# Transposing DMAs in place of fp32 TensorE transposes in a recurrent layer with routed experts

## The chip, the core and the metric

The kernel runs on one core of a Trainium2 chip. The metric is the device time of one execution in microseconds (us); lower is better. Engines are named as in the profile: PE is TensorE's matmul stream, PEld its weight loads, DVE is VectorE, ACT ScalarE, POOL GpSimd, SP SyncE. SPq, POOLq and ACTq are the instructions by which these engines issue DMAs.

## What is computed

4096 tokens (8 sequences of 512) of 256 channels are normalised. One branch is a linear recurrence with a gate, the other a mixture of 8 experts with the best two of them per token; the output is the input plus the product of the two.

```python
xn = _layernorm(x, axis=-1)
# recurrent branch, per sequence
q, v = xn @ Wq, xn @ Wv
new = sigmoid(beta) * prev + v_t            # over the 512 steps
y = layernorm(q * states) * ln_g + ln_b
s = (y * silu(xn @ Wg)) @ Wo
# expert branch
logits = xn @ router_weight.T; top 2 of 8, gates = softmax(top_vals)
o_e = (silu(a) * b) @ w_out[e].T            # a, b = split(xn @ w_in[e].T)
g = silu(sum_e gate_e * o_e + bias)
out = x + s * g
```

## The kernel before, in words

Every matmul on data runs in fp16 pairs: a number is split into a high half and a low half (value minus high half), and the helper `three` (L1067) issues high*high, high*low and low*high into the same PSUM bank. A matmul needs its operand with channels on the partitions, so token rows have to be transposed somewhere.

**Routing stage.** SP loads x in 8 groups of 4 tiles of 128 tokens into `xst` (L308), then the first four pieces of the expert weights (`load_w(0)`, L317), then it fills `y_dram` with the bias (L321, L323). Per group, DVE takes statistics (`stats_x`), POOL the reciprocal root (`rstd`), ACT normalises into `rows`, a buffer of 260 fp32 words a token: 256 channels and 4 words of data on the routing (`norm_x`, L566). PE transposes the rows of a group in fp32 by 8 matmuls with the identity into bank A or B (`transpose_x`, L1082), ACT casts the bank to fp16 into `xnT` (`high_xt`, L573), DVE subtracts to get the low half (`low_xt`, L745), and PE computes the logits (`route_x`, L1090). `xnT` is also the operand of the three projections of the recurrence. DVE's program has `choose(0)` (L769 to L782) and the split of the projection weights (L824) between the low halves of groups 4 and 5, and `count(0)` and `place(0)` between those of groups 5 and 6; after group 7 comes `choose(1)`, and then the recurrence.

**Recurrence.** Eight steps, one per sequence. POOL scatters the rows meanwhile to `slots_dram`, a list per expert, one indirect DMA per tile and choice (64 of them, L454): 14 at first, then 8 per step. SP brings the rest of the expert weights, ACT and DVE split them in high and low halves.

**Experts.** 32 blocks of 256 slots of one expert each (pairs), then 7 blocks of 128 (singles). For block b, SP waits until the buffer is free, reads the block's row number from `blk_row`, and loads 260 KB from `slots_dram` into `slot_in` (`load_slots`, L348). PE transposes the block in fp32, 4 matmuls with the identity into bank D (`transpose_slots`, L1195); ACT casts to fp16 (`high_slots`, L659), DVE makes the low half (`low_slots`, L978). PE's order for a pair is in `one_block`: first half of the hidden layer into bank A, the transposes of the next block, second half into bank B, then the output matmuls of the block before into bank C; 24 matmuls each. ACT (L667, L672) and DVE (L984, L988) make the activations between them. DVE multiplies the outputs by the gates (`gate_y`, L1003), POOL adds them to `y_dram` by indirect DMAs (L524), where each block's scatter waits until the one before has landed, since two blocks can hold the same token. POOL reads the routing words of each block in `meta` (L478 to L490).

**End.** When all scatters have landed SP loads `y_dram` (L380), ACT applies silu, DVE multiplies and adds, SP stores.

Of the kernel before, what the change touches and what calls it, by code (L numbers as in the profile page):

```python
# [33 lines left out]
P = 128  # L34
B, S, D = 8, 512, 256
T = B * S
NT = T // P
KD = D // P
TPC = S // P
CH = B  # L40
# [61 lines left out]
def build(nc, x, wq, wv, wg, wo, beta, ln_g, ln_b, router, w_exp, bias, out):  # L102
    ctx = ExitStack()
    with ctx:
# [19 lines left out]
        rows = rows_raw[:, :].rearrange("p (t r) -> p t r", r=ROW)  # L124

# [31 lines left out]
        slot_in = [part(rows_raw, SB * ROW).rearrange("p (s r) -> p s r", r=ROW) for _ in range(2)]  # L157
# [83 lines left out]
        slots_ps = [bankD[:, i, :].rearrange("p (k n) -> p k n", k=KD) for i in range(2)]  # L241
# [6 lines left out]

        first_slots_ps = [bankB[:, i, :].rearrange("p (k n) -> p k n", k=KD) for i in range(2)]

        def slots_ps_of(b, i):
            return first_slots_ps[i] if isinstance(b, int) and b < 2 else slots_ps[i]
# [11 lines left out]
        xt_ps, xt_hi_ready, xt_lo_ready = map(sem, ("xt_ps", "xt_hi_ready", "xt_lo_ready"))  # L264
# [14 lines left out]
        slot_t_ps, slot_hi_ready, slot_lo_ready, h_ps, y_ps, y_sb = map(  # L279
            sem, ("slot_t_ps", "slot_hi_ready", "slot_lo_ready", "h_ps", "y_ps", "y_sb"))  # L280
# [14 lines left out]
        slots_v = slots_dram.rearrange("(n p) r -> p n r", p=P)  # L295
        w_exp_v = w_exp.rearrange("p (n w) -> p n w", w=PIECE)
# [5 lines left out]
        def _(sp):  # L302
# [39 lines left out]
            def load_slots(b, i):  # L342
                if not isinstance(b, int) or b >= 2:
                    sp.wait_ge(slot_t_ps, b - 1)
                if not isinstance(b, int) or 2 <= b < PAIRS + 2:
                    sp.wait_ge(meta_ready, b - 1)
                row = sp.value_load(blk_row[0:1, bass.ds(b, 1)], min_val=0, max_val=E * REGION // P)
                sp.dma_start(slot_in[i][:, 0:units(b), :], slots_v[:, bass.ds(row, units(b)), :])\  # L348
                  .then_inc(slot_loaded[i], 16)

            def two(b):
# [10 lines left out]
                if isinstance(b, int) and b == X_EARLY + 1:  # L362
                    for n in range(SINGLES):
                        row = sp.value_load(blk_row[0:1, PAIRS + n:PAIRS + n + 1], min_val=0,
                                            max_val=E * REGION // P)
                        sp.dma_start(one_in[:, n:n + 1, :], slots_v[:, bass.ds(row, 1), D:ROW])\
# [21 lines left out]
        def _(pool):  # L388
# [83 lines left out]
            def meta(b, i, first):  # L472

                pool.wait_ge(slot_loaded[i], b * 8 + 16 if i == 0 else b * 8 + 8)
# [3 lines left out]
                pool.tensor_tensor(is_first[i][:, :], slot_in[i][:, :, D], e_b, ALU.subtract)\  # L478
# [7 lines left out]
                pool.tensor_tensor(gate_c[i][:, :], slot_in[i][:, :, D + 1], is_first[i][:, :], ALU.mult)\  # L486
                    .then_inc(pool_step, 1)
                pool.wait_ge(pool_step, b * 3 + n_meta + 3)
                pool.tensor_tensor(gate_c[i][:, :], gate_c[i][:, :], slot_in[i][:, :, D + 2], ALU.add)
                pool.tensor_copy(dest_f[i][:, :], slot_in[i][:, :, D + 3]).then_inc(meta_ready, 1)  # L490
# [56 lines left out]
        def _(act):  # L547
# [13 lines left out]
            def norm_x(g):  # L561
# [3 lines left out]
                for j in range(g * TPC, (g + 1) * TPC):  # L565
                    last = act.activation(rows[:, j, 0:D], xst[:, j, :], ACT.Identity,  # L566
# [15 lines left out]
            norm_x(0)  # L582

            act.wait_ge(cols_loaded, 48)
            act.activation(cols[:, 3, :], cols[:, 0, :], ACT.Tanh, scale=0.5).then_inc(lam_th, 1)
            for g in range(1, CH):
                norm_x(g)
                high_xt(g - 1, 1 - g % 2)
# [6 lines left out]
            high_xt(CH - 1, 1)  # L595
# [30 lines left out]
            def recur(c, convert=True, last=False):  # L626
# [10 lines left out]
                if last:  # L637
# [14 lines left out]
            def high_slots(b, i, first):  # L652
# [3 lines left out]
                elif not first:  # L656
                    act.wait_ge(h_ps, b * 2 - 2)
# [676 lines left out]
```

## Time and profile before

| | us |
|---|---|
| three runs | 511.03, 509.99, 511.35 |
| median of the runs | 511.03 |
| profiled execution: span from the first to the last instruction | 509.6 |
| PE busy in the span | 426.3 (84%) |
| POOL busy | 268.0 (53%) |
| DVE busy | 307.9 (60%) |
| ACT busy | 214.4 (42%) |

The profile gives the span of its execution; the time of that execution with what lies around the span is not listed apart, and the runs lie 0.4 to 1.8 us above the span. Rows of the trace are read so: start, duration, engine, line of the code, operation, output<-input, shape, count; in square brackets the idle time of the engine just ahead, and what ended it. For a DMA the row of the issuing engine is the time of the issue; the landing is given apart.

### The profile page before, as it was taken

The page shows a single profiled execution, that of the slowest core. Times are in us where ns is not written, and L with a number is a line of the kernel's source. Part 1 is how long each engine was busy: PE and PEld are TensorE (multiplying, and loading weights), DVE is VectorE, ACT ScalarE, POOL GpSimd, SP SyncE. Part 2 cuts the span into 40 slices and gives each one's busy share as a digit, 9 for nine tenths or more (in the row PEclk, how much of TensorE's full clock was granted, in tenths as well). Part 3 has the DMA queues.
Part 4 walks back from the last instruction along what each step waited for, and adds up shares of the span by engine and source line. Part 5 has one row for each costly group of instructions (what it writes and reads, how often), then busy time and mean ns, then how long its engine had stood idle before and what let it go on. Part 6 is the DMA issues. An engine that isn't in the chain of part 4 may idle for free.

```text
span 509.6 us, 12045 instructions
## 1 busy us (share of the span) xinstructions
PE 426.3 (84%) x3446; PEld 337.1 (66%) x3447; DVE 307.9 (60%) x605; ACT 214.4 (42%) x340; POOL 268.0 (53%) x501
## 2 busy tenths in 40 slices
PE   1757795998898899998999989999999999997000
PEld 1644352665557798887888878888888888664000
DVE  4898999899965545464445444545454545443077
ACT  4873273777756433333324233424342423232060
POOL 4726775788762055555555464646564655633200
PEclk9999997999999999999999999999999999999655
DMA  8892366566923226645434343434343434342498
GB/s 250 297 354 93 90 241 220 175 235 231 327 89 85 84 45 144 144 63 106 60 62 62 62 62 62 57 67 62 62 62 62 62 62 54 68 58 25 75 351 302
DMA packets 52692, 64.70 MB, mean 127 GB/s; under 512 B 5552, under 2 KB 47536, under 8 KB 52656
## 3 DMA queue, kind: packets, MB, share of 16 engines
q1 hardware_dynamic: 37712, 45.55, 29.1%
q0 software_dynamic: 13296, 17.83, 20.9%
q10 hardware_dynamic: 1664, 1.06, 0.7%
q8 instruction: 10, 0.16, 0.1%
q14 instruction: 10, 0.08, 0.0%
HBM read 40.02 MB, written 28.74 MB: 135 GB/s over the span
## 4 chain that ended last, share of the span: by engine, by line
PE 38%; DMA 18%; DVE 16%; issue 14%; POOL 8%; ACT 2%; SPq 2%; DVEq 1%; POOLq 1%; ACTq 0%
PE bankC L1071 14%; PE bankB L1071 12%; DMA y_dram<-rows_raw 11%; PE bankA L1071 8%; POOL slots_dram L454 4%; DMA rows_raw<-slots_dram 4%; PE bankD L1195 2%; DMA w_raw<-x_in 2%; DVE rows_raw L1003 2%; POOL stat L418 1%; DVE w_raw L918 1%; DVE w_raw L1049 1%; DVE work L909 1%; DVE bn L935 1%; DMA w_raw<-y_dram 1%
## 5 line engine op out<-in xcount | busy, mean ns | idle before, releaser
L524 POOL DMA_INDIRECT y_dram<-rows_raw x71 | 113.2, 1595 | 50.1 <-issue 31.1
L1071 PE MATMUL bankC<-w_raw,rows_raw 128*128 x852 | 99.5, 273 | 2.3 <-DVE rows_raw L1041 2.1
L1071 PEld LDWEIGHTS bankC<-w_raw,rows_raw 128*128 128x128 f16 x852 | 81.9, 98 | 14.2 <-issue 3.5
L454 POOL DMA_INDIRECT slots_dram<-rows_raw,pos_i x64 | 74.1, 1158 | 31.1 <-issue 20.2
L1071 PE MATMUL bankA<-rows_raw,w_raw 128*128 128x256 f16 x768 | 89.1, 273 | 1.2 <-DVE rows_raw L978 1.2
L1071 PE MATMUL bankB<-rows_raw,w_raw 128*128 128x256 f16 x768 | 89.1, 273 | 0.0
L1071 PEld LDWEIGHTS bankA<-rows_raw,w_raw 128*128 x768 | 75.1, 98 | 10.1 <-issue 1.4
L1071 PEld LDWEIGHTS bankB<-rows_raw,w_raw 128*128 x768 | 75.2, 98 | 8.3
L988 DVE TENSOR_TENSOR rows_raw<-rows_raw 128x512 f16<-128x512 f32 x64 | 44.3, 693 | 45.6 <-ACT rows_raw L672 45.6
L984 DVE SCALAR_TENSOR_TENSOR rows_raw<-rows_raw,bankA 128x512 f32<-128x512 f32 x32 | 22.0, 688 | 73.6 <-ACT rows_raw L667 73.6
L667 ACT ACTIVATE rows_raw<-bankA 128x512 f32<-128x512 f32 x32 | 19.1, 596 | 101.2 <-PE bankA L1071 101.2
L672 ACT ACTIVATE rows_raw<-rows_raw 128x512 f16<-128x512 f32 x64 | 40.3, 630 | 49.6 <-DVE rows_raw L984 49.6
L518 POOL TENSOR_TENSOR spare<-spare 128x1 f32<-128x1 f32 x32 | 6.2, 192 | 95.6 <-DVE rows_raw L1003 94.6
L1003 DVE TENSOR_SCALAR rows_raw<-bankC,rows_raw 128x256 f32<-128x256 f32 x71 | 31.4, 480 | 11.7 <-DMA y_dram<-rows_raw 9.4
L984 DVE SCALAR_TENSOR_TENSOR rows_raw<-rows_raw,bankB 128x512 f32<-128x512 f32 x32 | 22.0, 688 | 15.6 <-ACT rows_raw L667 15.5
L667 ACT ACTIVATE rows_raw<-bankB 128x512 f32<-128x512 f32 x32 | 19.1, 597 | 22.0 <-PE bankB L1071 22.0
L918 DVE SCALAR_TENSOR_TENSOR w_raw<-work,w_raw 128x1024 f32 (+1 forms) x24 | 27.7, 1214 | 0.0
L978 DVE TENSOR_TENSOR rows_raw<-bankD,rows_raw 128x512 f16<-128x512 f32 (+1 forms) x37 | 23.5, 634 | 2.5 <-ACT rows_raw L659 2.4
L1195 PE MATMUL bankD<-ident,rows_raw 128*128 128x128 f32 x134 | 21.4, 278 | 3.5 <-DMA rows_raw<-slots_dram 2.9
L1071 PE MATMUL bankC<-wat_hi,work 128*128 128x256 f16 x128 | 22.3, 273 | 1.8 <-DVE work L963 1.4
L645 ACT ACTIVATE work<-bankD,stat 128x256 f32<-128x256 f32 x32 | 15.4, 564 | 19.5 <-POOL stat L419 19.5
L478 POOL TENSOR_TENSOR rows_raw<-rows_raw,blk_e 128x2 f32<-128x2 f32 x32 | 23.5, 735 | 0.0
(181 smaller groups left out, 640.6 us busy)
## 6 DMA issues: line engine op xcount, KB each, us to landing
work<-w_exp_in SPq DMA_DIRECT2D x24, 512.0 KB, 5.0
rows_raw<-slots_dram SPq DMA_DIRECT2D x32, 260.0 KB, 2.8
w_raw<-x_in SPq DMA_DIRECT2D x9, 512.0 KB, 4.5
y_dram<-bias_in SPq DMA_DIRECT2D x4, 1024.0 KB, 12.7
w_raw<-y_dram SPq DMA_DIRECT2D x8, 512.0 KB, 7.4
out<-w_raw SPq DMA_DIRECT2D x8, 512.0 KB, 3.8
work<-x_in SPq DMA_DIRECT2D x7, 512.0 KB
slots_dram<-fill SPq DMA_DIRECT2D x9, 260.0 KB, 5.7
```

Of the source, the lines that this page charges most:

```text
L454: pool.indirect_dma_start(out=slots_dram, out_offset=bass.IndirectOffsetOnAxis(slot, 0), in_=row, in_offset=None, bounds_check=SLOTS - 1, ...
L478: pool.tensor_tensor(is_first[i][:, :], slot_in[i][:, :, D], e_b, ALU.subtract)\
L524: pool.indirect_dma_start(out=y_dram, out_offset=bass.IndirectOffsetOnAxis(to, 0), in_=ys[i][:, s, :], in_offset=None, bounds_check=ROWS_O ...
L667: act.activation(sil[j][:, :, 0:n], AB[j][:, :, 0:n], ACT.Silu, scale=1.0 / WSCALE).then_inc(sil_ready, 1)
L672: act.activation(g_hi[i][:, 2 * j:2 * j + 2, 0:n], g32[j][:, :, 0:n], ACT.Copy)\
L918: dve.scalar_tensor_tensor(w_lo[:, piece], wst[:, i % STAGES, :], WSCALE, w_hi[:, piece], ALU.mult, ALU.subtract).then_inc(w_lo_ready, 1)
L978: dve.tensor_tensor(xT[i][:, KD:2 * KD, 0:n], slots_ps_of(b, i)[:, :, 0:n], xT[i][:, 0:KD, 0:n], ALU.subtract).then_inc(slot_lo_ready, 1)
L984: dve.scalar_tensor_tensor(g32[j][:, :, 0:n], sil[j][:, :, 0:n], 1.0 / WSCALE, AB[j][:, :, BLOCK:BLOCK + n], ALU.mult, ALU.mult).then_inc( ...
L988: dve.tensor_tensor(g_lo[i][:, 2 * j:2 * j + 2, 0:n], g32[j][:, :, 0:n], g_hi[i][:, 2 * j:2 * j + 2, 0:n], ALU.subtract).then_inc(g_split, 1)
L1003: last = dve.tensor_scalar(ys[i][:, s, :], bankC[:, i, s * D:s * D + D], gates[:, s:s + 1], None, ALU.mult)
L1071: last = pe.matmul(out_ap, lhsT, rhs, start=(n == 0), stop=(n == len(todo) - 1))
L1195: last = pe.transpose(slots_ps_of(b, i)[:, k, s * P:s * P + P], slot_in[i][:, s, k * P:k * P + P], ident32[:, :])
```

## The change

Three edits that go together.

1. **Rows hold fp16 halves.** `norm_x` normalises `xst` in place. ACT (`high_x`) casts a group to fp16 into the first 256 halfwords of its rows, DVE (`low_x`) writes the low half into the next 256. A row keeps its 260 words, so the scatters move the same bytes.
2. **The projections' operand.** For each of the 8 groups SP waits for `low_x` and issues four transposing DMAs from the rows into `xnT`, 128 rows of 512 halfwords each (32 DMAs). PE's fp32 transposes and the casts out of PSUM are gone. The DMAs stand on SP between `load_w(0)` and the fills of `y_dram`.
3. **The expert blocks.** `load_slots` waits until the hidden layer of the block two before is done, and issues one transposing DMA from `slots_dram` straight into the operand `xT`, both halves; a second small DMA brings the 4 routing words (`meta_in`), for which SP waits for `meta` of the block two before. `transpose_slots`, `high_slots` and `low_slots` are gone.

```diff
+        rows16 = rows_raw[:, :].bitcast(F16).rearrange("p (t r) -> p t r", r=2 * ROW)
...
-        slot_in = [part(rows_raw, SB * ROW).rearrange("p (s r) -> p s r", r=ROW) for _ in range(2)]
+        meta_in = [part(rows_raw, SB * META).rearrange("p (s r) -> p s r", r=META) for _ in range(2)]
...
@@ sync
             load_w(0)
+
+            for g in range(CH):
+                sp.wait_ge(x_lo_ready, g + 1)
+                for j in range(TPC):
+                    sp.dma_start_transpose(xnT[:, g, :, j * P:j * P + P], rows16[:, g * TPC + j, 0:2 * D])\
+                      .then_inc(xt_loaded[g], 16)
+
             for t in range(0, NT, 2 * TPC):
...
             def load_slots(b, i):
-                if not isinstance(b, int) or b >= 2:
-                    sp.wait_ge(slot_t_ps, b - 1)
-                if not isinstance(b, int) or 2 <= b < PAIRS + 2:
-                    sp.wait_ge(meta_ready, b - 1)
-                row = sp.value_load(blk_row[0:1, bass.ds(b, 1)], min_val=0, max_val=E * REGION // P)
-                sp.dma_start(slot_in[i][:, 0:units(b), :], slots_v[:, bass.ds(row, units(b)), :])\
+                if isinstance(b, int) and b >= PAIRS + 2:
+                    sp.wait_ge(one_h_ps, b - PAIRS - 1)
+                elif not isinstance(b, int) or b >= 2:
+                    sp.wait_ge(h_ps, b * 2 - 2)
+                n = units(b) * P
+                row = sp.value_load(blk_row[0:1, bass.ds(b, 1)], min_val=0, max_val=E * REGION)
+                sp.dma_start_transpose(xT[i][:, :, 0:n], slots16[bass.ds(row, n), 0:2 * D])\
                   .then_inc(slot_loaded[i], 16)
+                if not isinstance(b, int) or b < PAIRS:
+                    if not isinstance(b, int) or b >= 2:
+                        sp.wait_ge(meta_ready, b - 1)
+                    sp.dma_start(meta_in[i], slots_dram[bass.ds(row, BLOCK), D:ROW]
+                                 .rearrange("(s p) r -> p s r", p=P)).then_inc(meta_loaded[i], 16)
...
@@ scalar
-                    last = act.activation(rows[:, j, 0:D], xst[:, j, :], ACT.Identity,
+                    last = act.activation(xst[:, j, :], xst[:, j, :], ACT.Identity,
...
-            def high_xt(g, i):
-                act.wait_ge(xt_ps, g + 1)
-                act.activation(xnT[:, g, 0:KD, :], AB[i][:, :, :], ACT.Copy).then_inc(xt_hi_ready, 1)
+            def high_x(g):
+                act.wait_ge(x_norm, g + 1)
+                tiles = slice(g * TPC, (g + 1) * TPC)
+                act.activation(rows16[:, tiles, 0:D], xst[:, tiles, :], ACT.Copy).then_inc(x_hi_ready, 1)
...
@@ vector
-            def low_xt(g, i):
-                dve.wait_ge(xt_hi_ready, g + 1)
-                dve.tensor_tensor(xnT[:, g, KD:2 * KD, :], AB[i][:, :, :], xnT[:, g, 0:KD, :],
-                                  ALU.subtract).then_inc(xt_lo_ready, 1)
+            def low_x(g):
+                dve.wait_ge(x_hi_ready, g + 1)
+                tiles = slice(g * TPC, (g + 1) * TPC)
+                dve.tensor_tensor(rows16[:, tiles, D:2 * D], xst[:, tiles, :], rows16[:, tiles, 0:D],
+                                  ALU.subtract).then_inc(x_lo_ready, 1)
...
@@ tensor
             def route_x(g):
-                pe.wait_ge(xt_lo_ready, g + 1)
+                pe.wait_ge(xt_loaded[g], 16 * TPC)
...
             def one_block(b, i, last=False):
                 off = weights_at(b)
-                pe.wait_ge(slot_lo_ready, b + 1)
+                slots_here(b, i)
                 hidden(b, i, 0, off, False)
-                if not last:
-                    transpose_slots(b + 1, 1 - i, False)
                 hidden(b, i, 1, off, False)
                 outputs(b - 1, 1 - i, weights_at(b - 1), False)
```

SP's queue at the start of the program, before (the loads of x stand ahead of these rows):

```order
L317 DMA work<-w_exp_in 128x1024 x4
L321 DMA y_dram<-bias_in 128x8x256 x4
L323 DMA y_dram<-bias_in 16x2048
L317 DMA work<-w_exp_in 128x1024 [waits w_lo_ready] x8
```

and now (the pair of rows L321 stands eight times, once per group):

```order
L314 DMA work<-w_exp_in 128x1024 x4
L321 DMA_TRANSPOSE xs_raw<-rows_raw 128x4x128 [waits x_lo_ready]
L321 DMA_TRANSPOSE xs_raw<-rows_raw 128x4x128 x3
L321 DMA_TRANSPOSE xs_raw<-rows_raw 128x4x128 [waits x_lo_ready]
L321 DMA_TRANSPOSE xs_raw<-rows_raw 128x4x128 x3
```

Thirty-two DMAs with eight waits on DVE stand now ahead of the fills of `y_dram` and of all later loads.

PE's loop over the pairs, at the end of the first half of the hidden layer (bank A) and the start of the second (bank B), before:

```order
L1071 MATMUL bankA<-rows_raw,w_raw 128x256
L1190 ISA
L1195 MATMUL bankD<-ident,rows_raw 128x128 [waits slot_lo_ready,slot_loaded1]
L1195 MATMUL bankD<-ident,rows_raw 128x128 x3
L1071 ISA [waits g_ready]
L1071 MATMUL bankB<-rows_raw,w_raw 128x256 x2
```

and now:

```order
L1053 ISA
L1053 MATMUL bankA<-rows_raw,w_raw 128x256
L1053 ISA [waits g_ready]
L1053 MATMUL bankB<-rows_raw,w_raw 128x256 x2
L1053 ISA
```

The four transposes and their wait for a load are gone from the middle of the block; PE waits for `slot_loaded` once, ahead of the first half.

SP's loop over the pairs, one block, before:

```order
L347 ISA [waits meta_ready,slot_t_ps]
L347 TENSOR_LOAD blk_row
L347 ISA x2
L348 ISA
L348 DMA rows_raw<-slots_dram 128x2x260
```

and now:

```order
L352 ISA [waits h_ps]
L352 TENSOR_LOAD blk_row
L352 ISA x2
L353 ISA
L353 DMA_TRANSPOSE rows_raw<-slots_dram 128x4x256
L357 REGISTER_ALU
L358 ISA [waits meta_ready]
L358 DMA rows_raw<-slots_dram 128x2x4
```

The load no longer waits for POOL, but for PE's second half of the hidden layer two blocks before; the wait for POOL stands behind it, ahead of the small load.

## Rows read from the trace of the kernel before

**Rows 1.** The page: the span.
```profile
span 509.6 us, 12045 instructions
```
**Rows 2.** Windows: stretch; length, busy us (instructions) of PE, PEld, DVE, ACT, POOL; clock; DMA.
```profile
10.60:42.90 32.30, 22.90 (x207) 17.69 (x208) 28.84 (x86) 23.59 (x38) 14.07 (x40) 1.00 0.84 278
42.90:57.90 15.00, 11.05 (x49) 4.84 (x48) 13.93 (x50) 4.91 (x6) 11.34 (x13) 0.89 0.28 100
181.10:428.20 247.10, 243.44 (x2205) 214.87 (x2203) 122.95 (x203) 85.20 (x146) 139.43 (x320) 1.00 0.43 72
470.90:509.60 38.70, 0.00 (x0) 0.00 (x0) 18.83 (x17) 8.46 (x8) 3.11 (x2) 0.56 0.80 241
```
**Rows 3.** Timeline of PE, one pair in the middle of the experts.
```profile
343.45 0.60 PE L1195 MATMUL bankD<-ident,rows_raw 128*128 128x128 f32 x4
343.89 2.78 PE L1071 MATMUL bankB<-rows_raw,w_raw 128*128 128x256 f16 x24
346.51 2.78 PE L1071 MATMUL bankC<-w_raw,rows_raw 128*128 x24
349.13 2.78 PE L1071 MATMUL bankA<-rows_raw,w_raw 128*128 128x256 f16 x24
351.87 0.66 PE L1195 MATMUL bankD<-ident,rows_raw 128*128 128x128 f32 x4
```
**Rows 4.** Chain that ended last (start, us, what): bank B of blocks 2 and 31.
```profile
181.12 2.62 PE bankB L1071 x24
...
428.21 2.62 PE bankB L1071 x24
```
**Rows 5.** Timeline of POOL, the scatter of one pair, then that of block 30.
```profile
350.39 0.19 POOL L518 TENSOR_TENSOR spare<-spare 128x1 f32<-128x1 f32 x1 [2.11 <-DVE rows_raw L1003]
...
353.40 1.58 POOL L524 DMA_INDIRECT y_dram<-rows_raw  x1 [0.31 <-issue]
...
434.45 0.19 POOL L518 TENSOR_TENSOR spare<-spare 128x1 f32<-128x1 f32 x1 [1.91 <-DVE rows_raw L1003]
```
**Rows 6.** Instructions by tile y_dram: time from issue to landing of its DMAs.
```profile
DMA to landing us min/median/max: 3.6/3.9/14.1
```
**Rows 7.** Timeline of SP: the first load behind the last scatter of the experts.
```profile
482.17 7.12 SPq L380 DMA_DIRECT2D w_raw<-y_dram  x8
```
**Rows 8.** Timeline of PE at the first blocks: transposes of blocks 0 and 1, first hidden matmuls.
```profile
157.08 1.04 PE L1195 MATMUL bankB<-ident,rows_raw 128*128 128x128 f32 x8
...
159.31 2.79 PE L1071 MATMUL bankA<-rows_raw,w_raw 128*128 128x256 f16 x24 [1.19 <-DVE rows_raw L978]
```
**Rows 9.** Instructions of L348 (duration ns min/median/max): SP's block loads, 260 or 130 KB.
```profile
L348 SPq DMA_DIRECT2D rows_raw<-slots_dram x39: 337/381/400, 152.6 to 452.2; - x39
...
DMA to landing us min/median/max: 2.1/2.8/3.1
```
**Rows 10.** Waits of SP's queue: engine, line, waited for: us, times, longest.
```profile
SPq L346 <- POOL rows_raw L490: 213.7, 30, 11.7
```
**Rows 11.** Timeline of SP at the start.
```profile
17.99 2.52 SPq L317 DMA_DIRECT2D work<-w_exp_in  x4
20.55 12.09 SPq L321 DMA_DIRECT2D y_dram<-bias_in  x4
```
**Rows 12.** Timeline of the routing stage: choose(0), low halves of groups 5 to 7, last logits.
```profile
28.81 0.41 DVE L769 TENSOR_REDUCE w_raw<-bankD 128x128 f32<-128x256 f32 x1
35.57 1.21 DVE L745 TENSOR_TENSOR xs_raw<-bankB,xs_raw 128x1024 f16<-128x1024 f32 x1
39.93 1.22 DVE L745 TENSOR_TENSOR xs_raw<-bankA,xs_raw 128x1024 f16<-128x1024 f32 x1
41.07 1.21 DVE L745 TENSOR_TENSOR xs_raw<-bankB,xs_raw 128x1024 f16<-128x1024 f32 x1
42.34 0.56 PE L1090 MATMUL bankD<-rt,xs_raw 128*128 128x16 f16 x16 [0.57 <-DVE xs_raw L745]
```
**Rows 13.** Timeline of POOL: one scatter of rows to the slots.
```profile
42.36 0.98 POOL L454 DMA_INDIRECT slots_dram<-rows_raw,pos_i  x1 [0.30 <-issue]
```

More of the change, by code:

```diff
@@ L263, in build @@
         bn_done, x_var, x_rstd, x_norm = map(sem, ("bn_done", "x_var", "x_rstd", "x_norm"))
[L264 removed]
+        x_hi_ready, x_lo_ready = sem("x_hi_ready"), sem("x_lo_ready")
+        xt_loaded = [sem(f"xt_loaded{g}") for g in range(CH)]
         logits_done, route_step, chosen_ready, ranks_done = map(
@@ L650, in recur @@
                     keep_s(c)
-            def high_slots(b, i, first):
-                act.wait_ge(slot_t_ps, b + 1)
-                if isinstance(b, int) and b >= PAIRS + 2:
-                    act.wait_ge(one_h_ps, b - PAIRS - 1)
-                elif not first:
-                    act.wait_ge(h_ps, b * 2 - 2)
-                n = units(b) * P
-                act.activation(xT[i][:, 0:KD, 0:n], slots_ps_of(b, i)[:, :, 0:n], ACT.Copy)\
-                   .then_inc(slot_hi_ready, 1)
             def half(b, i, j, before):
@@ L673, in half, with halves @@
                    .then_inc(g_hi_ready, 1)
-            def halves(b, i, before, last=False):
+            def halves(b, i, before):
                 half(b, i, 0, before)
-                if not last:
-                    high_slots(b + 1, 1 - i, before == 0)
                 half(b, i, 1, before)
@@ L1005, in gate_y, with halves @@
                 last.then_inc(y_sb, 1)
-            def halves(b, i, last=False):
+            def halves(b, i):
                 half(b, i, 0)
-                if not last:
-                    low_slots(b + 1, 1 - i)
                 half(b, i, 1)
-            low_slots(0, 0)
-            low_slots(1, 1)
             half(0, 0, 0)
@@ L1074, in _ @@
             pe.wait_ge(consts, 2)
-            def transpose_x(g, i):
-                pe.wait_ge(x_norm, g + 1)
-                if g >= 2:
-                    pe.wait_ge(xt_lo_ready, g - 1)
-                for j in range(TPC):
-                    for k in range(KD):
-                        last = pe.transpose(AB[i][:, k, j * P:j * P + P],
-                                            rows[:, g * TPC + j, k * P:k * P + P], ident32[:, :])
-                last.then_inc(xt_ps, 1)
             def route_x(g):
-                pe.wait_ge(xt_lo_ready, g + 1)
+                pe.wait_ge(xt_loaded[g], 16 * TPC)
                 for j in range(TPC):
@@ L1187, in weights_at, with slots_here @@
                 return pe.value_load(blk_off[0:1, bass.ds(b, 1)], min_val=0, max_val=(E - 1) * EW)
-            def transpose_slots(b, i, first):
+            def slots_here(b, i):
                 pe.wait_ge(slot_loaded[i], b * 8 + 16 if i == 0 else b * 8 + 8)
-                if not first:
-                    pe.wait_ge(slot_lo_ready, b - 1)
-                for k in range(KD):
-                    for s in range(units(b)):
-                        last = pe.transpose(slots_ps_of(b, i)[:, k, s * P:s * P + P],
-                                            slot_in[i][:, s, k * P:k * P + P], ident32[:, :])
-                last.then_inc(slot_t_ps, 1)
             def hidden(b, i, j, off, first):
```

82 lines of the change are left out of this document (28 added, 54 removed).

## The prediction, made before the changed kernel ran

> **What bounds the kernel now.** I read the windows by stage first. In the routing stage, 10.6 to 42.9 us, DVE is busy 28.8 of 32.3 us and PE 22.9; nothing is full, the stage is a relay through all engines. In the pairs, 181.1 to 428.2 us, PE is busy 243.4 of 247.1 us: half of the span (509.6 us) is PE alone [rows 1, 2]. The timeline of PE shows what it does there: three groups of 24 matmuls that follow each other at 2.62 us (343.89, 346.51, 349.13), then four transposes, then the next group [rows 3]. The chain of waits runs through these groups; between bank B of block 2 and that of block 31 lie 428.21 - 181.12 = 247.1 us, 29 blocks of 8.52 us [rows 4]. Three groups make 7.86 us, so transposes and what they wait for cost 0.66 us a block. Behind the pairs POOL decides: from the moment it takes up the scatter of block 30 (434.45) to the first load of the end (482.17) lie 47.7 us of scatters that wait for each other [rows 5, 7].
>
> **What the change takes away from the experts.** The four transposes of a pair go, with the wait for the load in the middle of the block, and the cast and subtraction behind them on ACT and DVE, which are off the path. If PE then runs group after group, 29 blocks x 0.66 = **19.1 us** go. At the first blocks PE transposes from 157.08 and starts the hidden layer at 159.31 [rows 8]; without the transposes it can start at once, 2.2 us earlier, and the two transposes ahead of bank B of block 2 (0.44 us each in the pitch of rows 3) go too: **3.1 us**. From block 30 on nothing is gained, since the scatters do not change: the 7 transposes of the singles are worth nothing while POOL's chain is the later one.
>
> What must hold for this. (a) The load of a block is now late by two conditions of its own: it starts when the hidden layer of the block two before is done, and must have landed when PE comes to its first half, that is after an output group, two hidden groups and an output group, 4 x 2.62 = 10.5 us. A plain load of these bytes lands 2.8 us after its issue [rows 9]; SP must also read the row number. Slack about 7 us. (b) SP waited 214 us for `meta` in these loads [rows 10]. That wait now stands behind the transposing DMA, and behind it only the small load of routing words and the next block's load are queued. The two DMAs per block cost SP twice 0.38 us instead of once, out of time that it spends waiting. (c) POOL's scatter of a pair begins at 350.39, issues its second DMA at 353.40, which lands 3.9 us later: 6.9 us before the next scatter can begin [rows 5, 6]. That fits under 7.86 us, by 1.0 us.
>
> **What it costs in the routing stage.** The casts and subtractions stay, 1024 elements a partition, now out of SBUF instead of PSUM; a subtraction took 1.21 us [rows 12] and I take the same. The fp32 transposes of PE go, but what stands in their place is on the path: 32 DMAs on one queue. SP is not free for them before 17.99 + 2.52 = 20.5 us [rows 11], where PE could transpose a group as soon as it was normalised. Call T the time by which a transposing DMA of 128 KB holds the queue. No row shows one. From below: SP issues a plain DMA in 0.38 us [rows 9]. From above, the dearest issue of 128 rows in the trace: POOL's indirect DMA, 0.98 + 0.30 = 1.28 us [rows 13]. The nearest by queue and bytes is the first; but a transposition must be cut into many more pieces than a copy of rows, as an indirect DMA is, so I take the middle, **T = 0.8 us**, and keep both ends.
>
> The relay then runs as follows; 2.1 us is the landing of 130 KB [rows 9], 1.7 us of it behind the issue. Low halves of groups 0 to 3 are ready by the time SP reaches them. 16 DMAs end at 20.5 + 16T, with landing and `route_x` (0.56 us [rows 12]) the logits of the first half are there at 22.8 + 16T = 35.6 us. Then DVE's order decides: today `choose(0)` starts at 28.81 and the low halves of groups 5, 6 and 7 end at 36.78, 41.15 and 42.28, that is 7.97, 12.34 and 13.47 us later [rows 12]; now they end at 43.6, 47.9 and 49.1. Group 5's four DMAs take SP from 43.6 to 46.8, group 6's from 47.9 to 51.1, group 7's to 54.3; with 1.7 + 0.6 the last logits are there at 56.6 us instead of 42.90. **+13.7 us**, and the recurrence begins that much later. With T = 0.38 the same sums give 46.6 (+3.7), with T = 1.28 they give 68.9 (+26.0).
>
> Behind SP's waits stand the fills of `y_dram` (12.1 us of issue [rows 11]) and the second piece of the expert weights. The fills are needed at the first scatter of the experts, 100 us later; the weights wait for DVE, which comes later as well. Both at nothing; cover gone, the fills would delay the weights by a few us.
>
> **The clock.** PE has little left to do in the routing stage. Where it idled at the end of the program, the granted clock was 0.56 on average; in 42.9 to 57.9 us, with 11.05 us busy of 15, it was 0.89 [rows 2]. Were that stretch run at the lower level (1.2 GHz, 0.5), PE's 11.05 us would become 11.05 x 0.89 / 0.5 = 19.7, 4.7 more than the stretch. Most of it lies beside `choose(1)` on DVE: I take **+1.5 us**, from 0 to 4.7.
>
> **Sum.** 509.6 - 19.1 - 3.1 + 13.7 + 1.5 = 502.6 us of span. The profiled execution's span lies 1.4 us under the median, so **504.0 us** against 511.03. The change balances a sure gain against an unknown T: it breaks even where the routing stage loses 22.2 - 1.5 = 20.7 us, at T = 1.1 us.
>
> The Trainium skill speaks on both sides. Its page "Advanced Engine Details and Errata", section "X-Bar Transpose (TRN2)", says that transposing DMAs are as fast as ordinary ones; by that T would be that of the plain issue, and the sum 493. Its page "DMA: Bandwidth & Descriptors" gives, in a table of the sequencer's own time, 631 cycles for a transpose out of HBM against 512 for a copy in earlier generations, but for a transpose out of SBUF one push per tile, so that its price grows with the data; it does not say there how large a tile is, so it gives no time here. That second rule speaks against exactly the 32 DMAs out of SBUF, not against the blocks, and no row here shows either.
>
> **The rivals.**
> 1. *SP becomes the bound of the routing stage.* If the queue takes a transpose out of SBUF piece by piece, T is over 1.1 us and all 32 stand in line on the path. It decides from T = 1.1. At T = 1.28: 509.6 - 22.2 + 26.0 + 1.5 + 1.4 = 516; at T = 1.6 (logits at 77.9, +35.0) 525; at 2.0 (89.1, +46) 536. For it: the issue of 128 single rows already costs 1.28 us on POOL. Against: SP's plain issue costs the same 0.38 us for 130 and 260 KB [rows 9]. Chances 0.22 up to 525, 0.08 beyond. The skill's table of the sequencer's time is the rule that would bring this about.
> 2. *As cheap as a plain DMA.* T under 0.6: 493 to 499 us. For it, the same 0.38 us. Chance 0.18.
> 3. *Balance.* T of 1.05 to 1.15, or a block gain cut short: within 0.3% (about what a measurement of this kernel can tell from no change) of 511. Chance 0.10.
> 4. *The blocks come late.* If a block's transposing DMA lands more than 10.5 us after PE has left the buffer, two buffers no longer suffice: each block then takes half of 5.24 + landing, and at 11.8 us the 8.52 of today are back; with the routing loss the total is 511 + 13.7 + 1.5 - 3.1 = 523. It needs four times the plain landing. Chance 0.07.
> 5. *The scatters become the bound of the pairs.* If the new DMAs slow their landing from 3.9 to 5.5 us, a pair takes 8.5 us and 19.1 us are not gained: 523. One landing of 14.1 us shows that they can be slowed [rows 6]; the loads of today move the same bytes beside them. Chance 0.05.
>
> **How the numbers follow.** The forecast proper, T from 0.6 to 1.05 with the blocks at 7.86 us, has 0.30 (498 to 510) and is the likeliest single case. With rival 2 that makes faster 0.48; same 0.10; slower 0.22 + 0.08 + 0.07 + 0.05 = 0.42. The range reaches from T = 0.38 without a cost of the clock (493) to T = 1.6 (525): it leaves out 0.08 and what of the rest falls outside, together under 2 in 10.
>
> **What would show it.** Right: the distance of bank B between pairs is 7.9 us; no ACT or DVE row on bank D or B between the hidden groups; the first hidden group starts as the last output projection of the recurrence ends. The rows of SP's transposing DMAs have a pitch of 0.8 us, and the last logits stand near 57 us. Wrong in the routing stage: SP's rows back to back at more than 1.1 us, with DVE idle ahead of `choose(0)` and PE waiting for a DMA. Wrong in the experts: PE waits for `slot_loaded` ahead of bank A, or DVE's `gate_y` for a landing on every block.

## The result, and the profile of the changed kernel

The changed kernel takes 522.01 us (median of 4 runs, 521.07 to 522.61) against 511.18 us of the kernel before on the same chip (4 runs): ratio 1.020, 95% interval 1.017 to 1.023. Its profiled execution has a span of 520.0 us, 10.4 more than before [rows 1]. The time lies in the range of 493 to 525, but on the side that I had not forecast: slower.

The page of the changed kernel, its first line:

```profile
span 520.0 us, 11470 instructions
```

Its windows in the routing stage and in the pairs (columns as in [rows 2]):

```profile
10.60:42.90 32.30, 1.76 (x48) 1.52 (x48) 16.08 (x54) 21.60 (x34) 16.84 (x38) 1.00 0.77 203
...
209.70:437.70 228.00, 228.00 (x2091) 204.37 (x2089) 105.44 (x174) 71.15 (x116) 146.95 (x319) 1.00 0.54 82
```

In the pairs PE is now busy without a gap. In the routing stage, where no engine had been full, DVE is down from 28.84 to 16.08 us of 32.3 and PE from 22.90 to 1.76: they wait. (The 1.00 for the clock in the first of these rows is taken up again under "Why the prediction was wrong".) The stage has moved to SP's queue. Timeline of SP:

```profile
17.84 1.99 SPq L314 DMA_DIRECT2D work<-w_exp_in  x4
19.86 49.56 SPq L321 DMA_TRANSPOSE xs_raw<-rows_raw  x32
69.47 7.14 SPq L325 DMA_DIRECT2D y_dram<-bias_in  x4
```

Instructions of L321, the DMAs out of SBUF (duration in ns min/median/max, first and last start in us), then of L353, those of the blocks, each with its time to landing:

```profile
L321 SPq DMA_TRANSPOSE xs_raw<-rows_raw x32: 1264/1267/2658, 19.9 to 68.2; - x32
...
DMA to landing us min/median/max: 2.4/2.5/8.6
```

```profile
L353 SPq DMA_TRANSPOSE rows_raw<-slots_dram x39: 1189/1263/1781, 183.8 to 466.1; - x39
...
DMA to landing us min/median/max: 2.6/3.8/4.4
```

A transposing DMA holds the queue for 1.27 us out of SBUF (128 rows of 512 halfwords) and for 1.26 us out of DRAM (256 rows, in the singles 128), where a plain one held it for 0.38 [rows 9]. The 32 stand from 19.9 to 69.4 us; the first four, behind the 2 MB of weights, take 7.9 us together. Behind them, the logits of groups 3 and 7 (timeline of PE) and the start of the two `choose` (timeline of DVE):

```profile
44.75 0.59 PE L1062 MATMUL bankD<-rt,xs_raw 128*128 128x16 f16 x16 [4.62 <-DMA xs_raw<-rows_raw]
...
71.85 0.60 PE L1062 MATMUL bankD<-rt,xs_raw 128*128 128x16 f16 x16 [4.90 <-DMA xs_raw<-rows_raw]
```

```profile
45.38 0.43 DVE L763 TENSOR_REDUCE w_raw<-bankD 128x128 f32<-128x256 f32 x1 [16.37 <-PE bankD L1062]
72.49 0.42 DVE L763 TENSOR_REDUCE w_raw<-bankD 128x128 f32<-128x256 f32 x1 [13.61 <-PE bankD L1062]
```

`choose(0)` starts at 45.38 instead of 28.81 [rows 12], the last logits end at 72.45 instead of 42.90: 29.5 us lost. The experts did what was forecast. Timeline of PE, the first hidden group and a pair in the middle; then the chain of waits, bank B of blocks 2 and 31:

```profile
188.32 2.78 PE L1053 MATMUL bankA<-rows_raw,w_raw 128*128 128x256 f16 x24
...
356.28 2.78 PE L1053 MATMUL bankA<-rows_raw,w_raw 128*128 128x256 f16 x24
358.90 2.78 PE L1053 MATMUL bankB<-rows_raw,w_raw 128*128 128x256 f16 x24
361.52 2.67 PE L1053 MATMUL bankC<-w_raw,rows_raw 128*128 x23
```

```profile
209.73 2.62 PE bankB L1053 x24
...
437.67 2.62 PE bankB L1053 x24
```

29 blocks in 437.67 - 209.73 = 227.94 us are 7.86 us each, against 8.52 [rows 4]: 19.2 us won. The whole sum, term by term:

| term | forecast | measured | from |
|---|---|---|---|
| pairs, blocks 3 to 31 | -19.1 | -19.16 | 227.94 against 247.1 |
| wait for the transposes ahead of the first hidden group | -2.2 | -2.23 | the group follows the recurrence at once; 159.31 - 157.08 before |
| transposes up to block 2 | -0.9 | -0.40 | 209.73 - 188.32 = 21.4 against 21.8 |
| routing stage | +13.7 | +29.55 | 72.45 against 42.90 |
| recurrence (the term of the clock) | +1.5 | +1.69 | 188.32 - 72.49 = 115.8 against 157.08 - 42.94 = 114.1 |
| block 31 to the end | 0 | +0.94 | 520.0 - 437.67 = 82.3 against 81.4 |
| sum | -7.0 | +10.39 | |

### The profile page after: what moved, and what is told of

It is laid out like the page before. It is cut to its first block, busy times and chain, and to the rows that moved or that the text cites. A ratio compares the mean times of both kernels' runs of the same rounds, so it can differ in the third digit from the quotient of the medians.

```text
span 520.0 us, 11470 instructions
## 1 busy us (share of the span) xinstructions
PE 399.8 (77%) x3240; PEld 313.1 (60%) x3241; DVE 285.8 (55%) x566; ACT 197.2 (38%) x301; POOL 281.0 (54%) x501
## 3 DMA queue, kind: packets, MB, share of 16 engines
q10 hardware_dynamic: 1664, 1.06, 0.7%
## 4 chain that ended last, share of the span: by engine, by line
PE 50%; DVE 14%; DMA 11%; issue 10%; POOL 7%; SPq 4%; ACT 3%; DVEq 1%; POOLq 0%; ACTq 0%
PE bankA L1053 17%; PE bankC L1053 17%; PE bankB L1053 16%; DMA y_dram<-rows_raw 6%; SPq L321 4%; POOL slots_dram L464 3%; DVE w_raw L912 2%; DMA w_raw<-x_in 2%; POOL stat L428 1%; DVE work L903 1%; DMA xs_raw<-rows_raw 1%; DVE w_raw L1031 1%; DMA w_raw<-y_dram 1%; ACT w_raw L576 1%; DVE bn L929 1%
## 5 line engine op out<-in xcount | busy, mean ns | idle before, releaser
L534 POOL DMA_INDIRECT y_dram<-rows_raw x71 | 114.4, 1611 | 50.1 <-issue 31.1
L1053 PE MATMUL bankC<-w_raw,rows_raw 128*128 x852 | 100.7, 275 | 2.7 <-DVE rows_raw L1023 2.6
L1053 PEld LDWEIGHTS bankC<-w_raw,rows_raw 128*128 128x128 f16 x852 | 83.5, 98 | 15.4 <-issue 4.4
L664 ACT ACTIVATE rows_raw<-bankA 128x512 f32<-128x512 f32 x32 | 19.1, 597 | 100.0 <-PE bankA L1053 96.6
L1062 PE MATMUL bankD<-rt,xs_raw 128*128 128x16 f16 x128 | 4.8, 175 | 56.0 <-DMA xs_raw<-rows_raw 56.0
L1062 PEld LDWEIGHTS bankD<-rt,xs_raw 128*128 128x128 f16 x128 | 4.2, 105 | 57.9 <-issue 30.2
L428 POOL TENSOR_TENSOR stat<-stat,neg_half 128x4 f32<-128x4 f32 x16 | 16.7, 1044 | 26.0 <-DVE stat L941 25.3
L664 ACT ACTIVATE rows_raw<-bankB 128x512 f32<-128x512 f32 x32 | 19.1, 597 | 17.5 <-PE bankB L1053 17.5
L1053 PE MATMUL bankC<-wat_hi,work 128*128 128x256 f16 x128 | 22.3, 273 | 2.1 <-DVE work L957 1.8
## 6 DMA issues: line engine op xcount, KB each, us to landing
y_dram<-bias_in SPq DMA_DIRECT2D x4, 1024.0 KB, 13.7
```

The source lines that it names most:

```text
L428: step(pool.tensor_tensor(stat[i][:, 1, :], stat[i][:, 0, :], neg_half[:, :], ALU.pow))
L534: pool.indirect_dma_start(out=y_dram, out_offset=bass.IndirectOffsetOnAxis(to, 0), in_=ys[i][:, s, :], in_offset=None, bounds_check=ROWS_O ...
L664: act.activation(sil[j][:, :, 0:n], AB[j][:, :, 0:n], ACT.Silu, scale=1.0 / WSCALE).then_inc(sil_ready, 1)
L1053: last = pe.matmul(out_ap, lhsT, rhs, start=(n == 0), stop=(n == len(todo) - 1))
```

## Experiments

Two theories of T, the time for which one transposing DMA holds SP's queue, were set against each other. F: a fixed price of 1.27 us for each. S: a price that goes with the data out of SBUF (1.27 us for 128 KB), so that the equal price of 256 KB out of DRAM is another rule. A third, D: DVE's order makes the loss, since `choose(0)` still stands ahead of the low halves of groups 5 to 7 and holds back their DMAs.

### e1: the same bytes in twice as many DMAs

```diff
-sp.dma_start_transpose(xnT[:, g, :, j * P:j * P + P], rows16[:, g * TPC + j, 0:2 * D])
+for h in range(2):
+    sp.dma_start_transpose(xnT[:, g, h * KD:h * KD + KD, j * P:j * P + P],
+                           rows16[:, g * TPC + j, h * D:h * D + D])
...
```

> The change with each of the 32 transposing DMAs out of SBUF cut in two (64 of 128 x 256 halfwords). Theory F, a fixed price on SP's queue for every transposing DMA: SP's rows keep 1.26 us each at a pitch of 1.31, the 64 stand from 19.9 to 104 us, the last logits move from 72.5 to about 106, the time from 522 to about 556. Theory S, a price that goes with the data out of SBUF: rows of about 0.64 us, the time stays at 522.

Measured: 556.28 us, one run. Instructions of the DMAs' line, then the second `choose` in the timeline of DVE:

```profile
L322 SPq DMA_TRANSPOSE xs_raw<-rows_raw x64: 1168/1247/2263, 19.7 to 103.2; - x64
```

```profile
106.27 0.42 DVE L765 TENSOR_REDUCE w_raw<-bankD 128x128 f32<-128x256 f32 x1 [28.99 <-PE bankD L1064]
```

Half the data costs 1.25 us where the whole cost 1.27, and the time is F's to within 0.3 us. S falls for sizes up to 128 KB.

### e2: the low halves first

```diff
 for g in range(CH):
     ...
     low_x(g)
-    if g == GC:
-        choose(0)
...
+choose(0)
...
+count(0)
+place(0)
 choose(1)
```

> The change with DVE's low halves of groups 5 to 7 ahead of choose(0) instead of behind it (and the gates of the first half behind the last normalisation on ACT). If the price of the DMAs alone makes the loss, SP never waits, the 32 DMAs end at 19.9 + 32 x 1.31 = 61.8 instead of 69.5, the last logits stand at 64.5 and the time falls by 8 us to 514: 22 of the 29.5 us are then the queue, 8 the order. If instead the order made it, the last logits would come near 57 and the time near 507. If the 7.5 us that SP waited for the low halves were hidden, 522.

Measured: 515.63 us, ratio to before 1.010 (1.006 to 1.014). The last logits:

```profile
67.84 0.59 PE L1059 MATMUL bankD<-rt,xs_raw 128*128 128x16 f16 x16 [4.42 <-DMA xs_raw<-rows_raw]
```

They come 4.0 us earlier than in the change, not 8. The 8 rested on what the waits of SP's queue list for the change (us, times, longest):

```profile
SPq L321 <- DVE rows_raw L739: 7.5, 3, 4.7
```

Only the longest of the three is a gap between two issues (48.72 to 53.40 us); the other 2.8 us lie beside issues that were already running. In e2 that gap is gone, but single issues are longer: the first four take 8.6 us instead of 7.9, and five take 7.44 from 53.2 us on. The span falls by 5.4 us (514.6 against 520.0), 4.2 of them by the first hidden group (184.17). So theory D falls (it had 57 us for the last logits), and the order is a lesser part of the 29.5 us; the queue alone is the greater.

### e3: one DMA per group

The halves of a group go into one stretch of SBUF that is free at that time (the expert weights come there later, so their casts wait for the copies as well); one DMA transposes 128 x 2048 halfwords, and eight plain DMAs copy the halves into the rows. e3o adds the order of e2.

```diff
-for j in range(TPC):
-    sp.dma_start_transpose(xnT[:, g, :, j * P:j * P + P], rows16[:, g * TPC + j, 0:2 * D])
+sp.dma_start_transpose(xnT[:, g, :, :, :].rearrange("p j q n -> p (j q) n"), halves_of[g])
...
+for g in range(CH):
+    sp.dma_start(rows16[:, g * TPC:(g + 1) * TPC, 0:2 * D], halves_by_tile[g])
...
```

> The change with the halves of a group in one stretch of SBUF, so that one DMA of 128 x 2048 halfwords transposes a group (8 instead of 32); 8 plain DMAs copy them into the rows. Theory F: 1.3 us each, choose(0) starts at 31 to 33 us instead of 45.4, the last logits at about 50 instead of 72.5, the time about 500. Theory S: 5.1 us each, 8 x 5.1 = 41 us as now, 522.

> The same with the low halves of groups 5 to 7 ahead of choose(0). Theory F: the low halves end near 38 us, the last logits near 43, but choose(1) still waits behind choose(0), the low half of the weights and the placing of the first half on DVE, so it starts near 49: within 3 us of the run before it, 497 to 502. Theory S: 514 as with the order alone.

Measured: 515.39 us (ratio 1.009, 1.006 to 1.012) and 507.18 us (0.993, 0.991 to 0.995). Instructions of the DMAs' line in e3, then its second `choose` in the timeline of DVE:

```profile
L324 SPq DMA_TRANSPOSE xs_raw<-w_raw x8: 1317/2367/8166, 20.7 to 52.8; - x8
...
DMA to landing us min/median/max: 4.2/4.7/10.2
```

```profile
58.87 0.42 DVE L774 TENSOR_REDUCE w_raw<-bankD 128x128 f32<-128x256 f32 x1 [6.28 <-PE bankD L1073]
```

Four times the data takes 1.32 us at best and 2.37 in the median, against 5.1 by S, which falls here too. But F does not hold as it stands either. Where the DMA engines had been idle just before (e3, e3q, e3r and e3s have such places), one issue took 1.32 us and four took 1.82 to 1.85, such as this one (timeline of SP in e3q):

```profile
38.72 1.84 SPq L322 DMA_TRANSPOSE xs_raw<-w_raw  x1
```

Where the engines were full (in e3o their busy share from 20 to 60 us is 1.02 to 1.10) the median is 2.70 us, and the DMAs land some 2.6 us apart: there the data seem to decide. The first issue of e3 stands for 8.2 us behind the 2 MB of weights issued just ahead.

Both forecasts missed. In e3 the last logits stand at 58.83 us instead of about 50, since eight issues at 1.3 us were too few. `choose(1)` still comes 13.6 us earlier than in the change, yet the time fell by 6.6 only: from `choose(1)` to the first hidden group it is 183.31 - 58.87 = 124.4 us instead of 115.8. That part I had left out: the copies are late, and POOL's scatters, which wait for them, start at 65.60 instead of 57.40.

### e3p, e3q, e3r, e3s: what the merged DMAs run into

e3p moves the first weights behind the transposes; e3q also moves `choose(0)` behind the low half of group 5, the cast of the projections' weights behind the last group, and the first weights between the fourth and the fifth copy.

```diff
-load_w(0)
 for g in range(CH):
     sp.wait_ge(x_lo_ready, g + 1)
     ...
+load_w(0)
```

> The change with one DMA per group and the low halves first, and the first weights (4 DMAs of 512 KB) behind the transposing DMAs on SP's queue instead of ahead. Theory: the first issue of 7.8 us and the first landing of 10.3 us are data that stand behind the weights in the DMA engines; without them the first four logits stand near 33 us instead of 38.5. Since choose(0) stands behind the last low half on DVE (39.9), the time falls by 2 us at most: 505 to 507. If the 8 us are a price of the first transposing DMA itself, the first landing stays at 10 us.

> The same with choose(0) behind the low half of group 5, and the projections' weights cast behind the last group (ACT and DVE). choose(0) starts at 32 to 34 us, the last low half ends near 40, with an issue of 1.4 to 2.7 us and a landing of 4 to 5 the last logits stand near 45 to 47 instead of 51, choose(1) starts there instead of at 52.1: time 499 to 502. If the DMA engines are the bound of the eight (2.5 us each from 20 us on, 8 x 2.55 = 20.4, so ended at 42), the same; if the halves' copies delay the first scatter and with it the recurrence, 505.

Measured: e3p 510.71 us (0.999, 0.997 to 1.001), e3q 502.47 (0.984, 0.980 to 0.987). In e3p the first logits come at 25.1 us and those of group 3 at 32.4. The first issue takes 4.0 us where it took 7.8 in e3o, and lands after 7.0 instead of 10.3, so about half of the 8 us were the weights' data. `choose(0)` still waits behind the low halves (39.91), as expected. But the time rose by 3.5 us over e3o, out of the expected range: the copies are later again, the first scatter goes at 59.26 instead of 56.25. e3q came within about 1 us of its forecast in the routing stage (`choose(1)` at 48.02) and in the time, and kept a recurrence of 123.0 us. Timeline of POOL in e3q:

```profile
53.81 1.25 POOL L471 DMA_INDIRECT slots_dram<-rows_raw,pos_i  x1 [21.48 <-issue]
...
73.18 1.05 POOL L434 TENSOR_TENSOR stat<-stat,neg_half 128x4 f32<-128x4 f32 x1
```

Fourteen scatters from 53.81 on stand ahead of the reciprocal root of the first step, whose variance DVE had ready at 63.15. e3r puts ten there and waits for the copies group by group; e3s moves the bias fills behind two more chunks of weights and scatters nine per step.

```diff
-SCATTERS_FIRST = 14
+SCATTERS_FIRST = 10
...
-pool.wait_ge(rows_copied[a // (TOPK * GT)], 16 * GC)
+pool.wait_ge(rows_copied[a // (TOPK * TPC)], 16)
```

> e3q with 10 instead of 14 scatters ahead of the first step of the recurrence, and waits for the halves' copies group by group (POOL's scatters, ACT's and DVE's weight pieces). In e3q the recurrence takes 123.0 us from choose(1) to the first hidden layer, 115.8 in the change itself. Theory: POOL starts its scatters at 53.8 instead of 40.8, the 14 hold the first 1/sigma until 74.3 where DVE had the variance at 63, and ACT waited until 66.5 for the last copies: 8 to 10 us go, recurrence at 114 to 116, time 493 to 496. Rival: the saturated DMA engines (busy share over 1.0 from 20 to 70 us) or PE's clock make the recurrence longer, then the time stays at 500 to 503.

> e3r with two waits taken away that it ran into: the bias fills of y_dram stand behind the weights of the second and third chunk on SP's queue (in e3r they held the second chunk until 76 us, its first cast waited 11.3 us until 87.8), and 9 instead of 8 scatters per step, so that none are left behind the last step (in e3r six were, and the first hidden layer waited to 175.3, with the output projection ended near 171). Theory: the second step's z comes at 79 to 80 instead of 94, the first hidden layer at 162 to 166, time 493 to 499. Rival: POOL with nine scatters a step becomes the bound of the recurrence (9 x 1.28 + 1.5 = 13.0 of 13.5 us), 500 or more.

Measured: e3r 509.08 us (0.994, 0.992 to 0.996), e3s 505.22 (0.986, 0.984 to 0.989). Both expectations missed. In e3r the first step's z came at 64.28 instead of 74.55, as meant, and the gain was gone one step later; the first cast of the second chunk of weights (timeline of ACT), and the first hidden group (timeline of PE):

```profile
87.78 1.06 ACT L634 ACTIVATE w_raw<-work 128x1024 f32 x1 [11.33 <-DMA work<-w_exp_in]
```

```profile
175.26 4.46 PE L1064 MATMUL bankA<-rows_raw,w_raw 128*128 128x256 f16 x24 [4.18 <-DMA rows_raw<-slots_dram]
```

The weights stood behind the bias fills on SP (issued up to 76.0 us), and six scatters were left behind the last step. After the 4.2 us for which PE then idled, its 24 matmuls took 4.46 us instead of the 2.78 of [rows 3], and the granted clock was 0.62 from 175.26 to 179.70. In e3s the second z came at 79.75 as forecast, but the fourth 22.3 us after the third (99.72, 122.02), with the fills now ahead of the fourth chunk of weights, and two later steps with nine scatters took 15 us each: the rival (500 or more) came out, with POOL as a part of the cause. These four point to SP's and POOL's queues, which had little room in the recurrence for what the merged path sends through them; how much each of the two took no run isolates.

### e4: the projections' operand back on PE

The expert blocks stay as in the change. PE transposes the normalised fp32 rows, ACT and DVE split out of PSUM as before, and the halves for the scatters are made aside: the high ones by ACT where it idles, the low ones by POOL (e4) or DVE (e4d, three ahead of `choose(1)`, five in the first two steps).

```diff
-for j in range(TPC):
-    sp.dma_start_transpose(xnT[:, g, :, j * P:j * P + P], rows16[:, g * TPC + j, 0:2 * D])
...
+last = pe.transpose(AB[i][:, k, j * P:j * P + P],
+                    xst[:, g * TPC + j, k * P:k * P + P], ident32[:, :])
...
+pool.tensor_tensor(rows16[:, tiles, D:2 * D], xst[:, tiles, :], rows16[:, tiles, 0:D],
+                   ALU.subtract)
...
```

> The change with the projections' operand back on PE's fp32 transposes (out of the normalised rows, cast and subtracted out of PSUM as before); the expert blocks stay as in the change. The halves of the rows are made aside: high by ACT where it idles, low by POOL (three groups ahead of the first scatters, one per step behind). If the loss sits in the routing stage alone, last logits are back at 43 to 46 us, the pairs keep 7.86 us, and the time is 511 - 2.2 - 0.4 - 19.1 = 489, plus what POOL's eight subtractions take from the scatters of the recurrence (no run shows their price; at 1.5 us each and no slack 8 us): 489 to 498. If part of the gain of the pairs hung on the new routing stage, 500 or more.

> The projections' operand through PE as in e4, with the low halves of the rows on DVE (1.2 us each) instead of POOL (2.1 us each, and choose(0) on DVE beside three of them took 9.3 us instead of 4.7). Theory: routing stage +3.6 us at most (three halves), recurrence +6 at most (five), and the pairs at 7.86 as before: 489 + 4 to 9.6 = 493 to 499. Rival: the slow choose(0) of e4 was not POOL's doing, then it is again at 38 us and the time at 504 or more.

Measured: e4 505.91 us (0.988, 0.985 to 0.992), e4d **498.76 us** (0.974, 0.972 to 0.976), the fastest of all. e4 missed its range of 489 to 498. Its `choose(1)` is 4.9 us later than before the change, and its recurrence 11.5 us longer (125.67 against 114.1). For the first of the two the rows show why. Timeline of POOL and timeline of DVE during `choose(0)` in e4:

```profile
30.14 6.37 POOL L454 TENSOR_TENSOR rows_raw<-w_raw,rows_raw 128x1024 f16<-128x1024 f32 x3
```

```profile
30.16 0.29 DVE L784 TENSOR_REDUCE w_raw<-w_raw 128x16 f32<-128x128 f32 x1
30.48 1.93 DVE L785 TENSOR_TENSOR w_raw<-w_raw 128x128 f32<-128x128 f32 x1
32.45 2.09 DVE L787 SCALAR_TENSOR_TENSOR w_raw<-w_raw 128x128 f32<-128x128 f32 x1
34.57 0.29 DVE L780 TENSOR_REDUCE w_raw<-w_raw 128x16 f32<-128x128 f32 x1
34.89 1.77 DVE L781 TENSOR_TENSOR w_raw<-w_raw 128x128 f32<-128x128 f32 x1
...
37.34 0.29 DVE L785 TENSOR_TENSOR w_raw<-w_raw 128x128 f32<-128x128 f32 x1
```

Three DVE instructions take 1.77 to 2.09 us, where L785 takes 0.29 once POOL is done (36.51): each ends within 0.15 us of one of POOL's three subtractions of 2.1 us. The two reductions beside them, which read one operand, keep their 0.29. In e4d, with POOL's subtractions gone, `choose(0)` has no such instruction. Its `choose(1)` (timeline of DVE), its first hidden group (timeline of PE), and bank B of two pairs that follow each other (chain of waits):

```profile
46.31 0.42 DVE L773 TENSOR_REDUCE w_raw<-bankD 128x128 f32<-128x256 f32 x1 [0.65 <-PE bankD L1088]
```

```profile
166.48 2.78 PE L1069 MATMUL bankA<-rows_raw,w_raw 128*128 128x256 f16 x24
```

```profile
187.88 2.62 PE bankB L1069 x24
195.74 2.62 PE bankB L1069 x24
```

Routing +3.4 us, recurrence 166.48 - 46.31 = 120.2, that is +6.0 over 114.1 (eight subtractions of 1.21 us make 9.7, the sum of both is 9.4), pairs 7.86. With -2.2, -0.4 and -19.2 of the table that is -12.4; the span, 496.8, is 12.8 below the one before. The recurrence is 5.5 us shorter than in e4, so POOL's subtractions cost more there than DVE's. The gain of the pairs hangs on nothing in the routing stage.

### e5: does SP have room in the pairs?

```diff
-sp.dma_start_transpose(xT[i][:, :, 0:n], slots16[bass.ds(row, n), 0:2 * D])
+for h in range(2):
+    sp.dma_start_transpose(xT[i][:, h * KD:h * KD + KD, 0:n],
+                           slots16[bass.ds(row, n), h * D:h * D + D])
...
```

> The change with the transposing DMA of each expert block cut in two (high and low half apart): 39 more DMAs at 1.26 us on SP. SP idled 137 us in these loads for PE (4.2 us a block), and PE has about 7 us from the release of the buffer to the next use: the pairs keep 7.86 us and the time stays at 522 (within 1). If SP's queue were near the bound of the pairs, 29 x 1.3 = 38 us more: 560; if the landing were near the bound, something between.

Measured: 523.72 us, one run. Instructions of the DMAs' line in e5; then the waits of SP's queue (waited for: us, times, longest) in e5 and in the change:

```profile
L354 SPq DMA_TRANSPOSE rows_raw<-slots_dram x78: 1167/1202/2440, 185.3 to 468.7; - x78
```

```profile
SPq L352 <- PE bankB L1055: 111.8, 32, 6.0
```

```profile
SPq L352 <- PE bankB L1053: 137.1, 33, 7.3
...
SPq L358 <- POOL rows_raw L500: 21.9, 15, 1.6
```

39 DMAs more, and bank B of the pairs still comes every 7.86 us; SP only waits less. The time is 0.7 us above the range that I had set; of the 2.0 us by which its span is longer than the change's, 1.6 lie ahead of the experts (first hidden group at 189.87 against 188.32). Nearly the same price that decides the routing stage costs the pairs nothing.

## Why the prediction was wrong

**The step that failed is the size of T in the routing stage.** I took 0.8 us, the middle between SP's plain issue (0.38) and POOL's indirect one (1.28); it is 1.27, with a pitch of 1.31. The middle had no row behind it, and with T = 0.8 the term came to +13.7 us where +29.55 was measured. I had reasoned that a transposition is cut into many pieces as an indirect DMA is. The pieces are there, in the DMA engines (pages of the kernel before and of the changed one):

```profile
DMA packets 52692, 64.70 MB, mean 127 GB/s; under 512 B 5552, under 2 KB 47536, under 8 KB 52656
```

```profile
DMA packets 106692, 68.88 MB, mean 132 GB/s; under 512 B 68640, under 2 KB 101536, under 8 KB 106656
```

But SP's price does not go with them: in e1 twice as many DMAs carry nearly the same packets (107716), and each holds SP for 1.25 us.

The Trainium skill has a figure that I did not use: its page "VectorE: DVE Perf Modes", section "The three transpose paths", gives 1309 ns for a DMA transposition of 128 x 128 in 16 bits. It does not say whether that is the time of the issue or the time to the landing. The issues here are near it (1.25 to 1.27 us, at two to eight times the data: e1, the change, the blocks), the landings are not (2.5 and 3.8 us in the median of the change). The sentence that I did quote, that transposing DMAs are as fast as ordinary ones, does not hold for the issue: 3.3 times the plain one. Nor does the price out of SBUF grow with the data up to 128 KB, as I read the second rule.

**Rival 1 is what happened**, T above 1.1 and all 32 in line. It gave 516 at T = 1.28, a span of 514.9 against the 520.0 measured. Of the rest, 3.5 us are in the last logits (72.45 against 68.9), 1.0 in the tail, 0.5 at the first blocks. With the pitch of 1.31 the sum of the prediction gives 69.8 us for the last logits. What is left, 2.7 us, is that `choose(0)` starts 1.6 us later than that sum has it (the first four issues, behind the weights, take 7.9 us instead of 5.2), and that the last DMA lands 2.4 us behind its issue instead of 1.7.

**Right:** the pairs, to 0.1 us, with the first two conditions: (a) the load lands after 3.8 us, within 10.5, and e5 adds a DMA without harm; (b) SP's wait for `meta` fell from 213.7 us to 21.9, and SP waits 137 us for PE. The wait ahead of the first hidden group went, 2.2 us. Of the two transposes ahead of bank B of block 2 I got 0.4 instead of 0.9 us. Rival 4 did not occur.

**Right by a hair:** condition (c), the scatters under 7.86 us. Timeline of POOL in the change, two scatters that follow each other; then the landing of the scatters from 340 to 430 us (instructions of L534):

```profile
350.86 0.19 POOL L528 TENSOR_TENSOR spare<-spare 128x1 f32<-128x1 f32 x1 [1.26 <-issue]
...
358.93 0.19 POOL L528 TENSOR_TENSOR spare<-spare 128x1 f32<-128x1 f32 x1 [1.58 <-DMA y_dram<-rows_raw]
```

```profile
DMA to landing us min/median/max: 3.7/4.2/4.9
```

They stand 8.07 us apart, and the second is released by the landing of the scatter before, not by DVE as in [rows 5]; over the 32 pairs the mean distance is 7.88 us. The landings that took 3.9 us [rows 6] reach 4.9 here. PE did not come to feel it, so rival 5 did not occur either, but the 1.0 us of room that the prediction counted is used up: a PE still faster in the pairs would have met POOL.

**Right, the clock:** the recurrence is 1.7 us longer, forecast 1.5 for a lowered clock. Compare PE behind `choose(1)`, each time in the timeline of PE before and then in the change: two of the projections' matmuls of 128 x 512, then the transposes of the first step:

```profile
42.76 0.59 PE L1071 MATMUL bankA<-xs_raw,wat_hi 128*128 128x512 f16 x2
```

```profile
73.53 1.06 PE L1053 MATMUL bankA<-xs_raw,wat_hi 128*128 128x512 f16 x2
```

```profile
53.77 1.09 PE L1170 MATMUL bankD<-ident,work 128*128 128x128 f32 x8 [1.74 <-DVE work L922]
```

```profile
83.62 1.80 PE L1139 MATMUL bankD<-ident,work 128*128 128x128 f32 x8 [3.48 <-DVE work L916]
```

The window of the second of these stretches in the change reads half of full speed, the lower level of 1.2 GHz (the same work before, 52.50 to 57.90 us, reads 1.00):

```profile
83.90:87.20 3.30, 3.30 (x13) 2.01 (x12) 3.12 (x15) 0.00 (x0) 0.00 (x0) 0.50 0.92 319
```

And DVE waits for it. Its second scan, before (timeline of DVE), and now:

```profile
57.90 2.32 DVE L909 TENSOR_TENSOR_SCAN work<-cols,bankA 128x512 f32<-128x512 f32 x2
```

```profile
89.02 2.33 DVE L903 TENSOR_TENSOR_SCAN work<-cols,bankA 128x512 f32<-128x512 f32 x2 [1.18 <-PE bankA L1053]
```

It starts 89.02 - 72.49 = 16.5 us behind `choose(1)` instead of 57.90 - 42.94 = 15.0: 1.6 of the 1.7 us are there, and stay to the end of the recurrence. The 1.5 us was a choice between 0 and 4.7, so that its size came out is in part luck.

The readings of 1.00 in the routing stage, in [rows 2] and above, do not fit the matmuls: two of 128 x 512 take 1.06 us at 35.98 before and at 53.55 in the change, as they do where the reading is 0.50, against 0.59 where it is 1.00 later on. So PE ran at the lower level there in both kernels, in the change for longer: up to 77 us, 4.5 us into the recurrence.

## What to carry to other kernels

Count a transposing DMA by the instruction: here 1.25 to 1.27 us of its queue, whatever it moves from 64 to 256 KB. Where a queue has room behind another bound (the pairs) it replaced PE's transposes for nothing; where 32 of them stand in a relay it costs their number times the price. Merging them gained some of that back (e3q, 0.984), leaving that part on PE more (e4d, 0.974). Whether a second queue for half of them would have helped, no run tried. And when two parts of a change have opposite signs, forecast each by itself and try it by itself: the half that won made the kernel faster by 2.6% (e4d), the whole made it slower by 2.0%.

## What I had not expected of the hardware

- The issue of a transposing DMA costs nearly the same for 64 and 128 KB out of SBUF and for 256 KB out of DRAM (1247, 1267 and 1263 ns in the median); at 512 KB it took 1.32 to 1.85 us with the DMA engines idle just before, and 2.7 us in the median with the engines full (e3o).
- DVE stood still for whole instructions of POOL (0.29 us became 1.77 to 2.09 in e4), where it read two operands, and not where it read one. The Trainium skill, page "SBUF — State Buffer", section "Who interferes with whom", calls what the two share an exclusive lock; the rows agree.
- PE idled most of the routing stage of the change (1.76 us busy of 32.3), and when it came to the projections its matmuls took 1.06 us for two instead of 0.59, up to 77 us. The clock that the windows read in that stage (1.00) did not show it; the durations of the matmuls did.
